# Two waits for landed scatters in a mixture-of-experts dispatch on one core

## The reference

```python
x = x + xattn(layernorm(x), ctx, ctx)   # 32 sequences of 64 queries, 1601 keys each; softmax, values, layer norm
x = x + attn(layernorm(x))              # 64 sequences of 32 tokens, 16 heads, 17 keys made by a length projection
x = x + ffn(layernorm(x))               # mixture of experts
# ffn: logits = flat @ router_w.T ; scores, idx = top_k(logits + router_bias, 2) ; scores = softmax(scores)
#      out  = sum over the 2 chosen of 16 experts of score * ((silu(flat @ gate_e) * (flat @ up_e)) @ down_e)
#      out += (silu(flat @ sh_gate.T) * (flat @ sh_up.T)) @ sh_down.T      # the shared expert, every token
```

## Time and profile before

| | us |
|---|---|
| median of 3 runs | 552.42 (551.97 to 553.71) |
| the profiled execution, whole | 553.32 |
| its span, first to last instruction | 551.4 |
| TensorE busy | 495.5 |
| GpSimd busy | 206.4 |
| mean granted clock of TensorE | 0.976 of full |

### The profile page before, as it was taken

How to read it: one execution, slowest core, us unless ns; L and a number is a source line. 1 busy time by engine, 2 the same in 40 slices (tenths; PEclk the granted TensorE clock), 3 DMA queues, 4 the chain that set the end, 5 groups by cost and what they waited for, 6 DMA issues and landing times.

```text
span 551.4 us, 14466 instructions
## 1 busy us (share of the span) xinstructions
PE 495.5 (90%) x5012; PEld 347.5 (63%) x5013; DVE 399.2 (72%) x1064; ACT 198.3 (36%) x605; POOL 206.4 (37%) x338
## 2 busy tenths in 40 slices
PE   7997999999999999999999999999785399999960
PEld 7764666666666666666656666666542268888840
DVE  3799799999999999999544788888564225555545
ACT  2344332343223332233313655564400035555500
POOL 4000314011222222222114777777777205656520
PEclk9999999999999999999999999999999599999995
DMA  7999579877978888973128997300123215544249
GB/s 281 353 341 315 173 230 295 287 212 227 296 255 273 291 288 282 295 257 108 40 82 257 307 290 237 96 2 21 50 96 107 77 48 160 156 147 124 83 152 304
DMA packets 67348, 108.83 MB, mean 197 GB/s; under 512 B 8115, under 2 KB 49125, under 8 KB 67304
## 3 DMA queue, kind: packets, MB, share of 16 engines
q1 hardware_dynamic: 60888, 97.83, 56.5%
q0 software_dynamic: 3792, 8.43, 4.4%
q10 hardware_dynamic: 2624, 1.97, 1.2%
HBM read 85.31 MB, written 24.85 MB: 200 GB/s over the span
## 4 chain that ended last, share of the span: by engine, by line
PE 56%; POOL 9%; issue 9%; DVE 9%; DMA 9%; ACT 4%; another core or an unknown queue 3%; SPq 1%; ACTq 0%; POOLq 0%; DVEq 0%
PE banks L1130 15%; PE banks L1106 14%; POOL expert_out L758 7%; DMA ring<-in_ctx_dram 7%; DVE ctxT L1634 3%; PE banks L1118 3%; PE banks L1065 2%; PE banks L1143 2%; PE banks L1469 2%; PE banks L1239 2%; PE banks L1246 2%; DMA xn_all<-expert_out 2%; PE banks L1151 2%; PE banks L1262 2%
## 5 line engine op out<-in xcount | busy, mean ns | idle before, releaser
L1634 DVE STREAM_TRANSPOSE ctxT<-ring 128x832 f32<-128x832 f32 x128 | 121.7, 1009 | 4.0 <-DMA ring<-in_ctx_dram 4.0
L1106 PE MATMUL banks<-ctxT,qT_all 32*64 32x416 f32 (+2 forms) x2048 | 93.2, 498 | 1.9 <-issue 1.1
L1130 PE MATMUL banks<-ring,prob 128*64 128x256 f32 (+1 forms) x832 | 93.6, 381 | 0.7 <-ACT prob L836 0.7
L1130 PEld LDWEIGHTS banks<-ring,prob 128*64 128x64 f32 (+1 forms) x832 | 58.5, 137 | 31.6 <-issue 4.2
L1106 PEld LDWEIGHTS banks<-ctxT,qT_all 32*64 32x64 f32 x2048 | 56.7, 131 | 29.9 <-issue 12.5
L636 POOL TENSOR_TENSOR var<-mv,eps 128x1 f32<-128x1 f32 x32 | 6.3, 198 | 167.4 <-DVE mv L1679 115.3
L758 POOL DMA_INDIRECT expert_out<-prob,dest x47 | 46.3, 986 | 51.3 <-issue 28.9
L849 ACT ACTIVATE prob<-banks,negmax 128x416 f32<-128x416 f32 (+2 forms) x80 | 41.1, 531 | 30.2 <-DVE negmax L1656 30.2
L1512 PE MATMUL banks<-ring,ctxT 128*128 x188 | 48.8, 382 | 0.3 <-ACT ctxT L984 0.3
L836 ACT COPY prob<-banks 128x512 f32<-128x512 f32 x64 | 27.6, 514 | 38.7 <-PE banks L1118 38.6
L2075 DVE TENSOR_TENSOR ctxT<-banks,ctxT 128x128 f32<-128x128 f32 x47 | 13.7, 292 | 37.8 <-ACT ctxT L987 26.4
(11 more groups left out here) (265 smaller groups left out, 947.1 us busy)
## 6 DMA issues: line engine op xcount, KB each, us to landing
ring<-in_ctx_dram SPq DMA_DIRECT2D x48, 1024.0 KB
qT_all<-q_by_pair SPq DMA_DIRECT2D x56, 128.0 KB, 8.9
rows_by_expert<-blank SPq DMA_DIRECT2D x8, 774.0 KB, 6.1
ctxT<-rows_by_expert SPq DMA_DIRECT2D x47, 129.0 KB
mid<-stage SPq DMA_DIRECT2D x31, 128.0 KB, 2.3
ring<-in_ctx_dram SPq DMA_DIRECT2D x16, 130.0 KB
ctxT<-mid SPq DMA_DIRECT2D x16, 128.0 KB, 3.7
qT_all<-mid SPq DMA_DIRECT2D x16, 128.0 KB, 3.8
```

Source lines behind the costliest of these rows:

```text
L1106: last = pe.matmul(S[a][64 * b:64 * b + 64, 0:KW[a]], q_rep[mine, r, c, 64 * b:64 * b + 64], ctxT[mine, c, b, 0:KW[a]], start=c == 0, stop ...
L1130: last = pe.matmul(U[64 * b:64 * b + 64, 0:D], probT[0:rows, k, 64 * b:64 * b + 64], ring[0:rows, r, b, k, :], start=k == 0, stop=k == KT)
L1634: dve.transpose(ctxT[:, c].rearrange("p b (k j) -> p (b k) j", j=Q), ring[:, r].rearrange("p b k c -> p (b k) c")[:, :, columns(c):columns ...
```

## The change

GpSimd gets two more waits. The first stands behind `shares(1)` and ahead of the wait for the second places: until `scattered` has reached 16 x 12, which is that all of columns 0 to 11 have landed. The second stands behind column 21 (`PAUSE` = 22 columns issued, ten of the last twenty): until all 22 have landed. The columns, their order and everything on the other engines are as before.

```diff
--- before.py
+++ after.py
@@ -60,6 +60,7 @@
     NOWHERE = TOPK * TOK
     ROW = D + 2
     FIRST = 4
+    PAUSE = 22
     PARTS = (0, 6, NG)
     PG = [b - a for a, b in zip(PARTS, PARTS[1:])]
     PC = max(PG) * TOPK
@@ -745,10 +746,13 @@
             scatter(range(4, TOPK * PARTS[1]))
 
             shares(1)
+            pool.wait_ge(scattered, 16 * TOPK * PARTS[1])
             pool.wait_ge(place_ready, 2)
             scatter(range(TOPK * PARTS[1], TOPK * (PARTS[1] + FIRST)))
             pool.wait_ge(place_ready, 3)
-            scatter(range(TOPK * (PARTS[1] + FIRST), NK - 3))
+            scatter(range(TOPK * (PARTS[1] + FIRST), PAUSE))
+            pool.wait_ge(scattered, 16 * PAUSE)
+            scatter(range(PAUSE, NK - 3))
             pool.memset(sent_mark[:, :], 0.0).then_inc(nearly_sent, 1)
             scatter(range(NK - 3, NK))
```

## The result

The changed kernel takes 545.95 us in the median of 4 runs (544.09 to 546.81), the kernel before 552.39 in the median of 4 (551.97 to 553.71): ratio 0.9854, 95% interval 0.9828 to 0.9881. The forecast was 543.3 in a range of 541.4 to 552.0. The profiled execution took 545.49 with a span of 543.6, against 553.32 and 551.4.

The account below looks back on a forecast made before the run. The prediction took the start of the expert stage, delayed by TensorE's late signals during scatters, as the bound. 9.8 us gained less 0.7 for the clock gave −9.1, so 544.2 profiled and 543.3 as median; range 541.4 to 552.

Parts of the forecast that it names:

- the mechanism: TensorE's signals reach VectorE and ScalarE ever later, up to 16.4 us, while GpSimd scatters unbroken; pauses keep them prompt.
- the first gap: Sign among GpSimd's scatters: 2.7 to 3.1 us from start to start before number 13, as before number 23.
- the two idle stretches of TensorE: Sign on TensorE: standing still 3.3 us before the marker and 4.0 before the first rows, given as 3 to 4.
- one warning: Sign for the whole kernel: signals all prompt but time down by less than 7 us means a pause costs more than taken.
- The pauses' price: GpSimd's scatters end later by +1.2 to +1.5 us for the first pause, +1.5 to +1.8 for the second; +2.8 taken.
- Rows: Start of the expert stage: first rows turned at 437.7 instead of 447.48, a gain of 9.8 us.
- The clock: TensorE's clock around the first rows: a fall to half rate costing 0 or 1.5 us, taken as 0.7.
- The forecast's own lower bound: Whole kernel: 541.8 us if TensorE's clock stays at 2.4 GHz and the waits cost their low end, +2.2.
- A (nothing relieved): Rival at the scatters: pauses relieve nothing and all from 434.59 on moves by 2.8, 555.2 us; chance 0.17.
- B (back within each run of ten): Rival at the scatters: signals late again after six scatters of a run, rows at 441 to 444, 546 to 550; chance 0.15.
- The argument for the length of run that does no harm: Scatters between pauses: runs of 12, 10 and 10 are shorter than the 14 before the first late signal.
- the strict reading: At the scatters: by the skill's rule they would not hold the readers up, and the pauses would only cost.

Follow-up runs that it names:

- one_18: The changed kernel with one pause, behind scatter 18, in place of the two; against the kernel before on a quick chip: 542.97 us, ratio 1.0007.
- first_only: The changed kernel without the pause behind scatter 22, only the one behind scatter 12 kept; 550.14 us, ratio 0.9917 against the kernel before on a slow chip.
- second_only: The changed kernel without the pause behind scatter 12, only the one behind scatter 22 kept; 551.14 us, ratio 0.9912 against the kernel before on a slow chip.
- gap_short: The changed kernel with each of its two waits replaced by one small unneeded GpSimd operation; 551.42 us in one run on a slow chip.
- one_18_third: One pause behind scatter 18 in place of the changed kernel's two, run on a slow chip; 543.83 us, ratio 0.9828 against the kernel before.
- none_awake: The kernel before plus five unread TensorE products behind the last quarter's gates, on a slow chip; 558.30 us, ratio 1.0081 against the kernel before.
- spaced: The kernel before, without pauses, plus a small GpSimd operation behind each of the last 20 scatters; 554.12 us in one run on a slow chip.

## Why the prediction was right, and where it was not

**Right: what bounds the kernel, and the mechanism.** On the chip of the first measurement TensorE's signals reach their readers late while scatters run without a break; with pauses they are prompt, and the scatters' end, then the landing of the first rows, binds. Most of what was named as a sign is in the profile: L979 at 415.15 and 416.86 (414.8 and 416.5 forecast, from a start 0.32 later), VectorE's product done at 421.04, L1473 in one piece until 427.17 (427.0), no unknown queue. Two signs are not: the first gap is 3.73 us and not 2.7 to 3.1, and the second of the two idle stretches of TensorE is 1.96 us and not 3 to 4. And one warning came true: all signals are prompt and the time fell by less than 7, so a pause costs more than was taken.

**The pauses' price: too small.** Forecast +2.8 for both. Measured 2.15 and 1.46 more from start to start, 3.6 in all; the second is at the low end of its 1.5 to 1.8, the first (1.2 to 1.5) was mis-sized by 0.65 and more. GpSimd was idle for 2.43 ahead of scatter 13 and for 1.76 ahead of 23. Pauses at the first place were 3.44, 3.53 and 3.73 from start to start in three profiles, those elsewhere 2.69 to 3.01 in six (and 4.74 once, in one_18). The same kernel on chip C, whose trace has the landings, shows which part it is: the landings took 2.52 and 2.65 us, near the 2.44 taken, but from landing to the next scatter it was 0.92 at the first place and 0.27 at the second, where 0.30 to 0.64 had been taken from the row at 382.26, in which GpSimd waited for its own copy and for no landing. At the first place the wait stands ahead of another one, for the places; that this second wait is the reason is argued only. The first load was issued 3.47 later than before, where 2.8 was forecast; 0.32 of it is a later start that was there ahead of the first pause.

**Rows: 438.44 against 437.7.** A gain of 9.04 in place of 9.8, nearly all of the difference from the first load (436.23 against 435.6).

**The clock: 1.32 in place of 0.7.** First rows to first send took 7.53, before 6.21. The fall was forecast; the price lay between the bounds of 0 and 1.5. The step that failed was the guess that half of it would be hidden behind the first turns' other waits. The clock also fell once more, which the forecast did not have: the eight records of the last gates took 5.40 us (431.08 to 436.48, granted clock 0.71 and 0.86) in place of 3.4. That they cost nothing is because the rows came later still; of the 3.4 us forecast between the last Silu (434.3) and the rows, 1.3 were left (437.12 to 438.44).

**Sum.** The forecast's own lower bound is 0.2 off its terms: 552.4 less 9.8 and less the 0.6 saved at +2.2 is 542.0, not 541.8. Measured, 9.04 less 1.32 is 7.72, and that is what the first send shows (453.69 to 445.97), the spans (7.8) and the whole (7.83, forecast 9.1). The medians lie 6.4 apart, as the profiled execution of before stands 0.9 above its median and that of after 0.5 below; the forecast carried only the first of these over.

**The rivals.** A (nothing relieved) and B (back within each run of ten) are excluded on chip A by its profile. B's mechanism exists: first_only shows it with a run of 20 in place of 10, and second_only within a run of ten, behind a pause that came too late. The argument for the length of run that does no harm (14 before the first late signal) held: 12, 13, 14, 14, 15 and 15 scatters in first_only, gap_short, before, one_18_third, second_only and none_awake, the last four counted from scatter 5. What the argument took for granted, that the profile of one execution on one chip speaks for the kernel, did not: nothing in the rows hinted at it, and a rival "there is nothing to relieve on another chip" was missing. On chip C it would have been the forecast: the change measured +2.9 us there. That the first chip was one with late signals was luck, in so far as the forecast of a gain is concerned.

**The rule weighed.** The Trainium skill (SBUF — State Buffer, "SBUF: two separate sides") says that a DMA cannot be slowed by a compute op or the reverse. The records agree so far as TensorE's own pace goes: beside the scatters its sums of quarters 1 and 2 are added every 0.86 us (32 records of L1473 in 7.07 us), as in the kernel before when the scatters were over. The rule says nothing of signals between engines, and these runs show that they are held up on some chips; so the strict reading, by which the pauses would only cost, failed on chip A and holds on C and D.

**Best version met.** One pause behind scatter 18: 0.9828 on a slow chip, 1.0007 and 1.0008 on two quick ones, where two pauses gave 0.9854 and 1.0057. The two were not run together on a slow chip.

## What to carry to other kernels

When a reader waits for an "unknown queue" although the product it needs has ended, compare the end of the product with the start of its reader: a growing difference means that the signal is late and not the work. Here it took a dozen scatters from GpSimd at 1.27 us each, and one break of 0.9 to 2 us over that pitch, before that length is reached, prevented it (0.9 in one run alone); a slower pace seems to do so too, but cost as much as it gave (554.12 against 555.07). Measure the kernel before on more than one chip before tuning against such a wait: on two of the four chips that are known to differ there was nothing to gain, and on the one of them where two pauses were run they cost 0.6%. Whether a trace had landing times for GpSimd's scatters told the two kinds of chip apart in all fourteen profiles.

## What the runs showed of the hardware

- The same program took 542.75 and 543.53 on chips C and D and 552.39, 554.07 and 555.07 on A, E and B (medians of 4 to 25 runs). In its profiles on A and D the difference is one stretch: TensorE's signals during GpSimd's scatters, prompt (0.04 us) on D, up to 16 us late on A. C and D on one side and A, B and E on the other also differ in the landings of scatters on record, 512 of 512 against 153 to 216 (386 in spaced).
- Once it has set in, signals pass one by one with gaps of 3.6, 6.3 and 6.3 us on chip A; when the scatters are over, those held come through together (from 434.59, 1.8 us after the first row load was issued).
- Among scatters at 1.83 us (one profile, chip B) no signal is late, and among the sends of the expert stage, at 1.6, no profile has a wait for an unknown queue.
- A scatter of 128 rows of 1032 bytes lands 2.6 us after its start in the median of the traces of C and D, mostly 2.4 to 3.1 and once 4.48.
- What path the signals and the scatters share, and what lies behind the mark that distinguishes the chips, stays open.
